# A fused attention and feed-forward kernel on one core: another order of all engines' work in the steady-state step

## The reference, cut to what matters

```python
def attn_layer(x, Wqkv, qs, ksc, Wo):            # 16 heads of 64
    q, k, v = split(x @ Wqkv)                    # 128 -> 3 x 1024
    q = rotary(l2norm(q) * qs); k = rotary(l2norm(k) * ksc)
    out = local_attention(q, k, v)               # windows of 32, each looks at itself and the one before
    return out @ Wo                              # 1024 -> 128
def ffn_layer(x, g, bln, W1, b1, W2, b2):
    xn = layernorm(x) * g + bln
    a, gate = split(xn @ W1 + b1)                # 128 -> 2 x 341
    return a * gelu(gate) @ W2 + b2
for i in range(6):
    x = attn_layer(shift_tokens(x), ...) + x
    x = ffn_layer(shift_tokens(x), ...) + x
```

## Time and profile before

| | us |
|---|---|
| median of 3 runs | 1679.32 |
| lowest and highest run | 1672.07, 1684.6 |
| the profiled execution | 1676.23 |
| its span | 1673.8 |
| PE, PEld busy | 1502.2, 1219.5 |
| DVE, ACT, POOL busy | 1225.2, 1318.1, 1279.0 |

### The profile page before, as it was taken

How to read it: one execution, slowest core, us unless ns; L and a number is a source line. 1 busy time by engine, 2 the same in 40 slices (tenths; PEclk the granted TensorE clock), 3 DMA queues, 4 the chain that set the end, 5 groups by cost and what they waited for, 6 DMA issues and landing times.

```text
span 1673.8 us, 68288 instructions
## 1 busy us (share of the span) xinstructions
PE 1502.2 (90%) x28656; PEld 1219.5 (73%) x28656; DVE 1225.2 (73%) x2372; ACT 1318.1 (79%) x4793; POOL 1279.0 (76%) x1541
## 2 busy tenths in 40 slices
PE   6588999899999899899999999989999989999985
PEld 4367777687777777777777877777777777878764
DVE  4667777877877877677878777777777777778752
ACT  3367878888888878778879888888797887888873
POOL 2379877978877978868779878788788798788760
PEclk9679999999999999999999999999999999999998
DMA  4011221112211112212112212111221112111111
GB/s 124 2 40 45 61 61 28 48 49 54 66 41 48 41 42 53 63 40 55 46 30 65 67 43 55 34 41 47 57 59 55 34 40 60 36 42 47 31 44 32
DMA packets 50879, 80.63 MB, mean 48 GB/s; under 512 B 8947, under 2 KB 16806, under 8 KB 50574
## 3 DMA queue, kind: packets, MB, share of 16 engines
q1 hardware_dynamic: 50574, 76.28, 16.5%
HBM read 18.62 MB, written 1.05 MB: 12 GB/s over the span
## 4 chain that ended last, share of the span: by engine, by line
PE 53%; ACT 31%; POOL 6%; DVE 5%; issue 5%; DMA 0%; SPq 0%; DVEq 0%; POOLq 0%
ACT pr L651 12%; PE ps L414 8%; ACT sq L617 5%; PE ps L391 5%; PE ps L398 5%; PE ps L442 5%; PE ps L452 4%; PE ps L483 4%; PE ps L424 4%; PE ps L392 4%; PE ps L393 4%; ACT pT L657 3%; ACT kT L642 3%; PE ps L408 3%; ACT qT L642 3%
## 5 line engine op out<-in xcount | busy, mean ns | idle before, releaser
L792 POOL TENSOR_TENSOR t<-t 128x512 f32<-128x512 f32 x384 | 498.7, 1299 | 213.0 <-DVE t L971 213.0
L651 ACT ACTIVATE pr<-ps,nmax 128x64 f32<-128x64 f32 x1536 | 477.7, 365 | 1.3 <-DVE nmax L986 1.3
L813 POOL TENSOR_TENSOR t<-t,rn 128x512 f32<-128x512 f32 x384 | 392.8, 1044 | 7.5
L651 ACT ACTIVATION_READ_ACCUMULATOR pr<-ps,nmax 128x1 f32 x1536 | 383.7, 259 | 0.0
L969 DVE TENSOR_TENSOR t<-ps,rope 128x512 f32<-128x512 f32 x384 | 263.2, 686 | 150.5 <-PE ps L398 76.2
L617 ACT ACTIVATE sq<-ps 128x512 f32<-128x512 f32 x384 | 242.3, 650 | 61.0 <-PE ps L393 60.5
L391 PE MATMUL ps<-w_hi,xt_hi 128*128 128x512 f32 x576 | 273.1, 474 | 15.2 <-DVE t L971 6.7
L948 DVE TENSOR_REDUCE sums<-sq 128x8 f32<-128x512 f32 x384 | 249.9, 667 | 19.6 <-ACT sq L617 19.6
L971 DVE TENSOR_TENSOR t<-ps,rope 128x512 f32<-128x512 f32 x384 | 261.5, 681 | 0.0
L393 PE MATMUL ps<-w_hi,xt_lo 128*128 128x512 f32 x576 | 232.5, 404 | 0.0
L392 PE MATMUL ps<-w_lo,xt_hi 128*128 128x512 f32 x576 | 231.8, 402 | 0.3 <-issue 0.3
(11 more groups left out here) (126 smaller groups left out, 2795.0 us busy)
## 6 DMA issues: line engine op xcount, KB each, us to landing
v_win<-v SPq DMA_DIRECT2D x384, 128.0 KB, 2.3
wqkv<-wqkv_in SPq DMA_DIRECT2D x36, 256.0 KB, 3.9
xsh<-xr SPq DMA_DIRECT2D x24, 224.0 KB
wo<-wo_in SPq DMA_DIRECT2D x6, 512.0 KB, 3.3
w<-w_in SPq DMA_DIRECT2D x6, 342.0 KB, 4.5
w<-w_in SPq DMA_DIRECT2D x6, 172.5 KB
x<-x_in SPq DMA_DIRECT2D x4, 256.0 KB, 4.2
out<-x SPq DMA_DIRECT2D x4, 256.0 KB, 2.7
```

What stands on the lines that cost most here:

```text
L651: i = A(pr[:, c, odd * SPAN:(odd + 1) * SPAN], ps[:, S_BANK[odd], c * SPAN:(c + 1) * SPAN], ACT.Exp, bias=nmax[:, odd, c:c + 1], accum_out ...
L792: G.tensor_tensor(t1[:, c, :], t1[:, c, :], t2[:, c, :], ALU.add).then_inc(qk_added[c], 1)
L813: G.tensor_tensor(w, w, rn[:, par(u), h2, a, :].unsqueeze(2).broadcast_to([P, 8, E]), ALU.mult).then_inc(done, 1)
```

## The change

Every engine's `step(s)` lists the same tasks in another order, with other lags where that follows: the value matmuls of a unit come at lag 2 and at the end of the step (before: lag 3, in the first half), V1 is projected at lag 0 and V0 at lag 1 (before: both at lag 1), and all six gate and value pieces are done in step lag 8, spread over it (before: two in step lag 8 and four at the start of step lag 9). The loop is one step shorter. One copy of a q half (Q0) and one of a v half move from ScalarE to VectorE, one copy of oT from VectorE to ScalarE. The banks are dealt out anew, and the waits fit the new order; new among them are the waits of both v copies for the value matmuls of unit u - 2, and that of `transpose_x` for `x_final`. On SyncE the shift of the tokens is at lag 5 for 7.

The core of the diff (what stands in the lists is cut to a part of each engine's):

```diff
-    QKV_BANK = [0, 1, 0, 1, 0, 1]
-    TQ_BANK = [4, 5, 5, 4]
-    TP_BANK = [5, 4]
-    GATE_BANK = [1, 0, 1]
-    VALUE_BANK = [0, 1, 0]
+    QKV_BANK = [1, 1, 0, 0, 0, 1]
+    TQ_BANK = [4, 4, 5, 5]
+    TP_BANK = [4, 5]
+    GATE_BANK = [0, 1, 1]
+    VALUE_BANK = [1, 0, 0]
...
-    FIRST_STEP, LAST_STEP = -7, 103
+    FIRST_STEP, LAST_STEP = -7, 102
...
-                run_quad(s, 7, shift_tokens)
-                run(s, 2, shift_v, 0)
-                run(s, 1, shift_v, 1)
+                run(s, 0, shift_v, 0)
+                run_quad(s, 5, shift_tokens)
+                run(s, 0, shift_v, 1)
...
             def copy_v(u, odd):
                 dve.wait_ge(qkv_ps[V0 + odd], u + 1)
+                if u >= 2:
+                    dve.wait_ge(o_ps, 4 * (u - 1))
```

More of the change, by code:

```diff
@@ L499, in step @@
[L499 to L509, removed]
@@ L533, in step @@
-                if due(s, 9):
-                    bank_free(s, (o_ready[1], 3), (x_updated, 4), (x_updated, 5), (x_updated, 6))
+                if live(s, 1):
+                    bank_free(s, (rope_done[K1], 1))
+                    bank_free_of_quad(s, f_h, 9, FCH)
+                    project(s - 1, V0)
+                if live(s, 1):
+                    bank_free_of_quad(s, f_xhT, 8, 1)
+                    transpose_qk(s - 1, Q0)
+                if live(s, 0):
+                    bank_free(s, (v_ready[1], 1))
+                    project(s - 0, Q0)
@@ new lines, in step @@
+                if live(s, 0):
+                    bank_free(s, (v_ready[0], 1))
+                    project(s - 0, Q1)
+                if live(s, 1):
+                    transpose_qk(s - 1, Q1)
+                if live(s, 3):
+                    bank_free(s, (o_ready[0], 3))
+                    output_projection(s - 3)
+                if live(s, 0):
+                    bank_free(s, (rope_done[Q0], 0))
+                    project(s - 0, K0)
+                if due(s, 8):
+                    bank_free(s, (rope_done[Q1], 0), (v_ready[0], 1), (v_ready[0], 2), (v_ready[0], 3), (v_ready[0], 4), (v_ready[0], 5))
+                    ffn_up_gate((s - 8) // QUAD, 0)
@@ L542, in step @@
[L542 to L548, removed]
+                    bank_free(s, (tq_ready[Q1], 1))
+                    transpose_qk(s - 1, K1)
@@ L681, in step @@
             def step(s):
[L682 to L686, removed]
+                run(s, 0, square, Q0)
+                run(s, 0, upper_w, Q0)
+                run(s, 1, upper_w, V1)
+                run(s, 3, copy_o, 1)
+                run(s, 0, square, Q1)
+                run(s, 0, upper_w, Q1)
+                run(s, 2, exps, 2)
+                run(s, 2, exps, 3)
+                run(s, 1, copy_qk, Q1)
                 run(s, 0, square, K0)
                 run(s, 0, upper_w, K0)
[L689 to L694, removed]
+                run_quad(s, 8, ffn_gate, 0)
                 run(s, 1, copy_qk, K0)
[L696 to L699, removed]
+                run_quad(s, 8, ffn_gate, 1)
+                run(s, 1, copy_qk, K1)
                 run(s, 0, square, K1)
                 run(s, 0, upper_w, K1)
-                run(s, 2, exps, 3)
-                run(s, 0, square, Q1)
-                run(s, 0, upper_w, Q1)
-                run(s, 1, copy_qk, Q1)
-                run(s, 1, copy_qk, K1)
+                run_quad(s, 8, ffn_gate, 2)
+                run(s, 2, copy_pT, 0)
+                run_input(s, 9, copy_xt)
                 run_quad(s, 7, ffn_normalise)
                 run(s, 0, guess_norm)
-                run_quad(s, 8, ffn_gate, 0)
-                run_input(s, 9, copy_xt)
+                run(s, 2, copy_pT, 1)
+                run(s, 1, exps, 0)
+                run(s, 1, exps, 1)
+                run(s, 0, upper_w, V0)
+                run(s, 2, copy_o, 0)
+                run_quad(s, 7, ffn_upper)
             act.wait_ge(ld_const, 80)
@@ L960, in rotary @@
             def rotary(u, c):
-                if c in (Q0, K0, K1):
+                if c in (Q0, K0, Q1):
                     dve.wait_ge(sq_ready[c], u + 1)
-                if u >= 1 and c in (Q0, K0):
+                if u >= 1 and c in (K0, Q1):
                     dve.wait_ge(tq_ps[c], u)
```

177 lines of the change are left out of this document (86 added, 91 removed).

## The result

The changed kernel is slower: 1748.67 us (median of 4 runs, 1745.02 to 1756.38) against 1681.96 for the kernel before beside it (1672.07 to 1685.36). The ratio is 1.0421, 95% interval 1.0388 to 1.0454, or about 71 us. The forecast was 1690, and the time lies above its range of 1645 to 1728. The profiled execution has a span of 1749.4 us against 1673.8, and a mean granted clock of 0.963 against 0.972.

The account below looks back on a forecast made before the run. It took the beat to be bound by TensorE waiting for ScalarE's copies between scores, plus late fetches. Terms +3, +10 and -2 sum to +11: 1676.2 becomes 1687, the median 3 higher, forecast 1690 us, range 1645 to 1728.

Parts of the forecast that it names:

- What bounds the kernel: Whole loop: 16.07 us per unit; TensorE waits for ScalarE's 10.7 us run between scores; 27 late-fetch stops cost 45.6 us.
- The walk, +3: Four-unit loop, new order walked: 61.15 us per quad against 61.0, times 23.5 quads, +3 us.
- light step: The step with s mod 4 = 2: two loops of 13.0 us each, taken as 13.1 against 13.5.
- step 1: Step (s mod 4 = 1) with the down-projection: VectorE is the path, 16.5 us; row-maximum interval about 16.8.
- step 0: Step (s mod 4 = 0) with all six up-projections: 17.8 us; row-maximum interval about 18.3.
- step 3: Step (s mod 4 = 3) with four normalising activations before the second pT copy: 13.75 us; row-maximum interval about 13.1.
- The fetches, +10: TensorE's value matmuls: instruction blocks now arrive late in 54 units, 0.2 us each, 10 us, bounds 0 and 103.
- That loss stays: Fetch stops inside the scores: about as many block edges late in the scores, 42 after and 43 before.
- The ends, -2: Loop ends: one step fewer, 102 for 103, so the tail gives -2 us, between -5 and 0.
- The added waits, zero: v copies and SyncE's queue: zero; 0.3 us per unit (+29) if uncovered, up to 2 us per quad if order slips.
- Rival A: Value matmuls' fetch: the block edge costs 0.8 us in 54 units, so slower, 1723 us; chance 30%.
- B: Whole quad: moved pieces fill TensorE's holes, quad 59.7 us, -31 us, so faster, 1646 us; chance 25%.

Follow-up runs that it names:

- wo_opair: wo_first plus ScalarE's second o copy moved to right behind the first, at the end of the step: 1683.89 us, ratio 1.0037 to the kernel before.
- tok_last: wo_opair with the token shift put behind both v shifts of its step on SyncE's list: 1684.64 us, ratio 1.0010 to the kernel before.
- wo_first: Changed kernel with SyncE's load of the next layer's wo issued ahead of its step's two v shifts: 1718.58 us, ratio 1.0252 to the kernel before.
- opair_only: Changed kernel with only ScalarE's second o copy moved right behind the first, wo's load left late: 1720.33 us, ratio 1.0222 to the kernel before.
- the two edits meant to fill the walked holes: On wo_opair: K0 transposes ahead of gate 0, 1702.44 us; VectorE's low part of the transposed input behind the row maximum, 1695.75 us; both, 1728.70 us.

## Why the prediction was wrong

**What bounds the kernel.** Right. Unit beat, long steps and stops were read as they are, and the loss is in the beat.

**The walk, +3.** Right where nothing disturbs a step. wo_opair, which has the two late waits repaired, gives for the light step 13.0 for 13.0, and into step 1 a median of 16.9 for 16.8. Into step 0 ten of its 24 intervals lie between 18.4 and 18.9 for 18.3; those with a stop in the scores or at the end of a layer are longer, and the mean is 19.5. Into step 3 the undisturbed ones take 13.4 for 13.1, the median is 14.4. The chain shows one of the long ones (start, us, what):

```profile
428.44 1.74 issue
430.18 0.41 PE ps L415 x17
...
432.10 2.75 PE ps L443 x96
```

It is a stop in the scores and then value matmuls at 2.75 us for 1.53; the granted clock was 0.68 in 430 to 434. The interval behind this stop is 14.7 for 13.4. So this stop cost 1.74 us where it stands, and 1.3 more behind it, nearly all in those slower matmuls. But only two of the 24 intervals into step 3 hold half clock. Five have a stop of 0.6 to 1.5 us in the values and take 13.9 to 14.7, and five more, one in each layer from the first to the fifth, have a wait of 1.0 us for the copy of qT and take 15.4 to 16.1. The kernel before has its own disturbances: undisturbed it takes 13.5 there, and its median is 15.0.

Two of the prediction's terms are a little off. Its list of TensorE's work per unit adds up to 12.0 us, not 12.2. And VectorE's busy time grew by 0.84 us per unit for the 0.60 said, ScalarE's fell by 0.37 for 0.49. The interval of 13.0 came as walked all the same.

**The fetches, +10.** The mechanism came as told: the wait table has 21 stops in the values with 15.5 us for 4 with 2.5. Into step 3 such a stop costs about what it lasts (1.1 us of stop, 14.4 for 13.4); in the light step the short ones cost nothing. "That loss stays", said of the stops in the scores, held for the changed kernel (40.8 us for the 45.6 of the earlier trace rows) and not for wo_opair (27.6), where the two kinds together are 41.1 us for 48.1 in the kernel before. Rival A's price, 43 us, is not in the time.

**The ends, -2.** The row maxima begin 2 us later and the tail is 3 us longer: +5 for -2, small.

**The added waits, zero.** This is the first step that failed, in its part on SyncE. The prediction says of them "so zero", for the v copies because V0 and the Q0 transposes cover the copy, and for SyncE because the v shifts behind the token shift are needed a step later. Each sentence holds for what it names: tok_last is no faster. But it followed the queue one instruction too short. Behind the v shifts stands the load of wo, and the shifts now wait for V0, which is projected in the next step, two projections and two sets of transposes ahead of the output projection that needs wo. Measured: 28 us by wo_first, 31 between opair_only and wo_opair. The question "what is queued behind the waiting instruction" was asked for TensorE's data and not for every item of SyncE's list.

**The o copy, not priced.** This is the second. The walk of the light step names ScalarE's "square, copy, square" and never asks when TensorE reaches the output projection. It does so before that copy ends, in all four steps. In step 2 VectorE's loop hides this, and that is the step which was walked most closely. Measured: 36 us by wo_opair and 34 by opair_only, both with what the stops gave back.

The two make 64 of the 71 us. What is left is 0.4% in wo_opair, 0.1 to 1.1% over the four kernels with both repairs (wo_opair, tok_last and the two with added matmuls): 2 to 19 us, for the +11 forecast. So the sum is within what was measured for the kernel without those two waits, in part by luck: the stops in the scores, taken as unchanged, fell by 18 us in wo_opair. Which part of that remainder is the walk and which the fetches stays open, since moving the edges alone shifts it by up to 12 us.

Of the rivals, A named the right side for a reason that is not borne out. B did not happen, and the two edits meant to fill the walked holes moved a wait or went with more stops. The sign to look for in the profile was written down, "SyncE's held queue showing as values that wait for a DMA"; it showed, as the output projection waiting for a DMA.

## What to carry to other kernels

When a wait is added on one engine, write out everything behind each instruction it delays, down to loads that are issued once a layer: five loads, each some 10 us late, cost 28 us, and a test that delayed them in the kernel before held up the token shift as well. Walk every engine's arrival at every shared value in every kind of step; a light step that another loop limits hides a wait that the heavy steps pay. And before trusting half a per cent of an order, shift the instruction stream without changing the loop: here this alone moved the time by up to 12 us.

## What the runs showed of the hardware

- The load of wo took 3.2 to 3.3 us from issue to landing in the kernel before, 3.4 to 4.8 in the changed one, behind the v shifts, and 3.8 to 5.4 in wo_first, ahead of them. So its place behind them is not what makes it longer.
- Behind the wait of 5.8 us shown, the granted clock was 0.50 for the next 5 us, and 16 matmuls took 3.76 us for 1.78. The five waits for wo were 5.1 us on average, and the intervals that hold them 6.8 us longer than in wo_first: the price of such a wait was more than its length.
- Every stop for "issue" in the scores stands at the same place of a block of 256 TensorE instructions, in eight traces, and moved to other units when 32 or 64 matmuls were added ahead of the loop.
- In the four kernels with both repairs the profiled time went with the sum of the stops in scores and values, not with their number (41 or 42 in each): sums of 36.7, 41.1, 45.7 and 51.1 us, times of 1679.3, 1679.9, 1690.1 and 1701.2. Their time at half clock was 30.7, 20.5, 23.9 and 44.4 us.
